# A norm over masked scores: squares stored in 64 columns per set, two sets to a weight load

## The reference

```
h   = relu(layernorm(x))
q, k, v = h Wq^T, h Wk^T, h Wv^T
rel = adj^T * (q k^T)                        # 64 x 64 for each graph
rel = rel / norm(rel, over a node's row)     # the step that changes
x   = x + rel v
h   = relu(layernorm(x))
3 times:                                     # a gated step
    a = adj h                                # in_mat = out_mat = adj
    z = sigmoid([a, a] w3^T + b3 + h u3^T + bu3)
    r = sigmoid([a, a] w4^T + b4 + h u3^T + bu3)
    c = tanh([a, a] w5^T + b5 + (r * h) u5^T + bu5)
    h = (1 - z) h + z c
out = x + h
```

## Time and profile before

| | |
|---|---|
| runs (median, lowest, highest) | 991.85, 991.76, 992.97 us |
| profiled execution | 993.66 us, its span 991.8 us |
| TensorE matmuls busy | 973.6 us, 98% of the span |
| VectorE, ScalarE, GpSimd busy | 668.4, 500.2, 78.6 us |
| mean granted TensorE clock | 0.989 of full speed |
| norm products | 64 matmuls in 128 passes, 244 ns mean |
| Squares | 16 of 128 x 512, 616 ns |
| norm copies | 16 of 128 x 4, 158 ns |

### The profile page before, as it was taken

One profiled execution on the slowest core, in us unless ns is written; L12 is line 12 of the kernel. 1 busy time (PEld: TensorE's weight loads), 2 busy tenths in 40 slices (PEclk: granted clock), 3 DMA queues, 4 the chain that ended last, 5 costly groups with the idle time before them and its releaser, 6 DMA issues.

```text
span 991.8 us, 15059 instructions
## 1 busy us (share of the span) xinstructions
PE 973.6 (98%) x5368; PEld 843.2 (85%) x5368; DVE 668.4 (67%) x1338; ACT 500.2 (50%) x877; POOL 78.6 (8%) x90
## 2 busy tenths in 40 slices
PE   7899999999999999999999999999999999999996
PEld 7788888888888888888888888888888888888885
DVE  4766767766676675867757766776667766676645
ACT  4446554545445463554735645356444556445542
POOL 1210101100010000100001000100101101010000
PEclk9899999999999999999999999999999999999998
DMA  5011000211002010210101101021000211000001
GB/s 166 1 43 43 36 7 22 64 42 42 0 31 76 21 42 0 85 42 0 42 21 63 42 0 42 21 63 42 23 20 21 63 42 42 0 21 22 1 1 43
DMA packets 31457, 34.75 MB, mean 35 GB/s; under 512 B 3280, under 2 KB 29648, under 8 KB 31440
## 3 DMA queue, kind: packets, MB, share of 16 engines
q1 hardware_dynamic: 31440, 34.52, 10.7%
HBM read 18.78 MB, written 15.73 MB: 35 GB/s over the span
## 4 chain that ended last, share of the span: by engine, by line
PE 96%; DVE 1%; ACT 1%; DMA 1%; issue 0%; POOL 0%; SPq 0%; DVEq 0%
PE gate L333 13%; PE gate L335 13%; PE gate L334 13%; PE cand L333 9%; PE cand L335 9%; PE cand L334 9%; PE fea L436 8%; PE tok L429 4%; PE fea L396 3%; PE tok L333 2%; PE tok L334 2%; PE tok L335 2%; PE fea L333 1%; PE fea L334 1%; PE fea L335 1%; PE tok L445 1%
## 5 line engine op out<-in xcount | busy, mean ns | idle before, releaser
L839 DVE TENSOR_TENSOR d_s<-c_s,h 128x512 f32<-128x512 f32 x96 | 65.1, 691 | 72.4 <-ACT c_s L711 72.4
L692 ACT ACTIVATE r_s<-gate,b_r 128x512 f32<-128x512 f32 x96 | 65.1, 685 | 91.2 <-PE gate L335 91.2
L839 DVE TENSOR_TENSOR a_lo<-fea,a_hi 128x512 fp32r<-128x512 f32 x96 | 64.6, 688 | 47.4 <-ACT a_hi L621 47.4
L711 ACT ACTIVATE c_s<-cand,b_c 128x512 f32<-128x512 f32 x96 | 64.8, 684 | 51.1 <-PE cand L335 51.1
L839 DVE TENSOR_TENSOR rh_lo<-rh,rh_hi 128x512 fp32r<-128x512 f32 x96 | 66.6, 734 | 26.4 <-ACT rh_hi L621 25.1
L621 ACT ACTIVATE h_hi<-h 128x512 fp32r<-128x512 f32 x64 | 39.5, 633 | 88.3 <-DVE h L965 88.3
L621 ACT ACTIVATE a_hi<-fea 128x512 fp32r<-128x512 f32 x96 | 57.8, 603 | 42.8 <-PE fea L436 42.3
L333 PE MATMUL gate<-a_hi,W_hi_wz 128*128 128x512 f32 x192 | 79.1, 412 | 0.0
L333 PE MATMUL cand<-a_hi,W_hi_w 128*128 128x512 f32 x192 | 78.9, 411 | 0.0
L333 PE MATMUL cand<-rh_hi,W_hi_u 128*128 128x512 f32 x192 | 78.2, 407 | 0.0
L971 DVE TENSOR_TENSOR rh<-r_s,h 128x512 f32<-128x512 f32 x96 | 63.7, 682 | 19.5 <-ACT r_s L692 19.5
(11 more groups left out here) (117 smaller groups left out, 2271.1 us busy)
## 6 DMA issues: line engine op xcount, KB each, us to landing
x_s<-x SPq DMA_DIRECT2D x16, 512.0 KB, 4.6
out<-o_s SPq DMA_DIRECT2D x16, 512.0 KB, 3.0
hx_trip<-hx SPq DMA_DIRECT2D x14, 512.0 KB, 2.6
hx_back<-hx_trip SPq DMA_DIRECT2D x56, 128.0 KB, 2.8
z_s<-w_t SPq DMA_DIRECT2D x1, 512.0 KB, 4.0
r_s<-w_t SPq DMA_DIRECT2D x1, 512.0 KB, 4.9
c_s<-w_t SPq DMA_DIRECT2D x1, 512.0 KB, 5.8
rh<-u_t SPq DMA_DIRECT2D x2, 256.0 KB, 6.2
```

The lines of the kernel that those rows point to most:

```text
L692: nc.scalar.activation(r_s[:, c, :], gate[:, c, :], ACT.Sigmoid, bias=b_r[:, c:c + 1]).then_inc(r_ready, 1)
L711: nc.scalar.activation(c_s[:, c, :], cand[:, c, :], ACT.Tanh, bias=b_c[:, c:c + 1]).then_inc(c_ready, 1)
L839: return nc.vector.tensor_tensor(dst, a, b, ALU.subtract)
```

## The change

`sq` keeps only the two wanted blocks: 128 partitions x 4 sets x 64 columns. Each half of the partitions is squared by an instruction of its own. Two sets then lie side by side as 128 columns and are loaded as one stationary operand, and the moving operand is `of_half`: two columns, of which column 0 is one on partitions 0 to 63 and column 1 is one on partitions 64 to 127. So the sum for set q = 2b + a and graph e of it, which stood on partitions of half e in column q, now stands on partitions of half a in column 2b + e. Four small copies bring them to where `rnorm` is read.

```diff
+        of_half = sb("of_half", [P, 2])
...
-        sq = sb("sq", [P, Q, P])
+        sq = sb("sq", [P, Q, N])
...
+        def half(e):
+            return slice(e * N, (e + 1) * N)
...
-                for q in range(Q):
-                    last = nc.tensor.matmul(fea[:, 1, q:q + 1], sq[:, q, :], ones[:], start=True, stop=True)
+                for b in range(HQ):
+                    two = sq[:, 2 * b:2 * b + 2, :].rearrange("p q n -> p (q n)")
+                    last = nc.tensor.matmul(fea[:, 1, 2 * b:2 * b + 2], two, of_half[:], start=True, stop=True)
...
-                nc.scalar.activation(sq[:], S[:], ACT.Square).then_inc(sq_ready, 1)
+                for e in range(2):
+                    last = nc.scalar.activation(sq[half(e), :, :], S[half(e), :, half(e)], ACT.Square)
+                last.then_inc(sq_ready, 1)
...
-                nc.vector.tensor_copy(norm2[:], fea[:, 1, 0:Q]).then_inc(fea_taken, 2)
+                for e in range(2):
+                    for a in range(2):
+                        last = nc.vector.tensor_copy(norm2[half(e), :].rearrange("p (b a) -> p b a", a=2)[:, :, a],
+                                                     fea[half(a), 1, 0:Q].rearrange("p (b e) -> p b e", e=2)[:, :, e])
+                last.then_inc(fea_taken, 2)
...
+            for e in range(2):
+                for a in range(2):
+                    nc.vector.memset(of_half[half(a), e:e + 1], 1.0 if a == e else 0.0)
             statistics(0, 0, 0, 1)
```

## The result

The change made the kernel slower: 1001.59 us (997.89 to 1003.6, four runs) against 992.41 us (four runs; three of them had given the 991.85), a ratio of 1.0087 (95% interval 1.0064 to 1.011). The forecast was 985.7 us, faster. The steps of the forecast that concern the norms came out near their numbers; what failed is that one added tile of two columns, where it was declared, made the large products slower, in every window of the kernel.

The account below looks back on a forecast made before the run. TensorE's matmuls were taken to bound the loop, VectorE the early start-up. Loop -6.2, start-up +0.57 and -0.44 make -6.1 us, from the 991.85 us median to 985.7 us; 8-in-10 range 983.5 to 988.5.

Parts of the forecast that it names:

- rival 4: Large tiles moved in SBUF by the new tile: 2 ns more per 512-column product cancels the gain; chance 0.03.
- TensorE's saving: Norm products on TensorE: eight passes become four, saving 0.444 us a group, 6.2 us over the loop's 14 groups.
- The whole sum: Whole kernel: -6.2 us in the loop, +0.57 and -0.44 us in the start-up, together -6.1 us.
- The Squares: ScalarE: one Square becomes two of some 0.41 us, overlapping by 0.09; the pair ends 0.1 us later, hidden in the loop.
- Rival 1: Loop norms: Squares end 0.47 us late, stalling TensorE 0.13 us in each of 14 groups; 987.5 us, chance 0.08.
- The copies: VectorE: one norm copy becomes four at 0.16 us each, hidden in the loop with 0.4 us narrowest margin.
- The start-up: Before the loop: group 0 costs 0.57 us (Squares 0.1, copies 0.47), group 1 saves 0.44 us on TensorE.
- Rival 2: Start-up or tail: half-clock stretches fall elsewhere, giving 984.0 or 987.4 us, at the outside 982.3 or 989.1; chance 0.12.

## Why the prediction was wrong

- **The step that failed** is rival 4, *the moved tiles*, which was given 0.03 with "no row links speed to place" and left out of the sum. The prediction had the mechanism and its break-even, 2 ns for each of the 3,072 products of 512 columns. The runs showed 5.0 ns each on average: 15.4 us in all (1007.67 against 992.31), or 1.92 us a round. Added to the forecast of 985.7 that is 1001.1 us, and 1001.59 was measured. What it had wrong was the reason to put the term at nothing: the rows of before could not speak, because there every streamed tile lay a multiple of 256 bytes from the weights. That the distance to the weights decides was not in it.
- **TensorE's saving** was right: 0.444 us a group forecast, 0.45 measured; a round of 118.4 forecast, and 118.37 measured once the tiles lay as before.
- **The whole sum** (-6.1 us) was right for the change without its side effect: 6.16 us less up to the last transposes, in two executions whose start-ups had the same half-clock stretches. The medians gave -5.2 and -5.4 us with the tile of 256 bytes, -7.9 and -7.8 with the tile last; these take in whatever half-clock stretches each execution met.
- **The Squares** were forecast to overlap by 0.09 us. They start 0.41 us apart, 402 and 414 ns long and without overlap, and end 0.2 us later than one did. The 0.39 us that were free covered it, and 0.21 were left. Rival 1 did not happen. Whether the overlap goes with 64 partitions or with the change of half, no run tells.
- **The copies**: by the row 0.64 us, measured 0.70. Second, third, fourth and the next instruction started 0.16, 0.34, 0.51 and 0.70 us behind the first, each some 0.01 to 0.03 us after the one ahead had ended, so all four were held. With the rule of the Trainium skill that the prediction gives ("VectorE: DVE Perf Modes", "Two Vector instructions with no wait between them") the trace agrees: for the three later copies at each of the 16 places, for the instruction behind them at the nine where it waits for nothing else (at the seven of window 5 it waits for GpSimd). No run made such copies within one half, so that they would have overlapped there is not shown. In the loop they were hidden, by a margin that the doubled copies measured: with 0.68 us more, 0.50 us a round come through, so 0.18 us were free in window 5. The prediction had 0.4.
- **The start-up**: from norm to norm it grew by 0.78 us, the first 20.10 us apart with the tile last (24.32 to 44.42) where it was 19.32 (25.66 to 44.98); 0.57 was forecast. The instruction behind the Squares started 0.32 us later (0.85 us behind the first Square, where it had been 0.53 behind the one), and the last copy ended 0.50 us later than the one had (0.66 and 0.15 us behind the first start). Together that is 0.8 us, so it is the Squares' 0.1 us that was too small.
- **Rival 2**, the clock, did move the start-up, by some 4 us in the profiled pair. It was given 0.12 as a rival, but it is a spread that every forecast of this kernel needs: 982.6 to 988.0 us for the same code, the changed kernel with the tile last.

## What to carry to other kernels

In this program a new tile moves every tile that is declared behind it. Put small additions last, or keep the distance of streamed operands from their weights as it was, and compare the spacing of the large matmuls (here 226.7 ns) before and after any edit. A small gain can hide behind such a side effect, so before a change is thrown away, run it with the old addresses.

## What the runs showed of the hardware

- The rate of fp32r products of 512 columns, each with its own weight load, depends on the distance in SBUF between the stationary and the moving operand. At multiples of 256 bytes (0, 256, -256, 512) they settle at starts 226.7 ns apart, at 64 bytes about 229, at 32, 128 and 192 bytes 232 to 233. Once settled, moving both alike by 32, 64 or 128 bytes changes nothing. A start off the 32-byte grid cost 4 to 5 ns at 16 bytes and 10 to 11 ns at 4 bytes, whether the weights moved along or not. Shorter streams lose less at 32 bytes: 3 ns at 384 columns, and nothing at 504, which no theory here explains. That weight loads and streamed reads get in each other's way in SBUF would explain it, since the load of the next weights runs beside the stream; no run here took one of the two away, so this cause is argued and not shown.
- The 1.6% of time that it costs stays invisible in waits, busy shares and the granted clock: TensorE is busy for the whole round either way.
- ACTIVATEs of 64 partitions whose second one starts at partition 64 don't overlap (0.41 us apart, the first 402 ns long), nor does the tanh behind them (0.44 us behind the second, which takes 414 ns).
